# Three graph-attention layers on one core: accumulators kept per head in 28-word rows, heads turned by VectorE, products over padded head rows, index lists loaded early

## What is computed

```python
h = (x @ W).reshape(N, H, C)
alpha_s = einsum('nhc,hc->nh', h, a_src); alpha_d = einsum('nhc,hc->nh', h, a_dst)
e = leaky_relu(alpha_s[src] + alpha_d[dst], 0.2)
m = segment_max(e, dst);  ex = exp(e - m[dst]);  den = segment_sum(ex, dst)
out = segment_sum(h[src] * (ex / (den[dst] + 1e-16))[:, :, None], dst) + b
x = relu(out)                                   # three times
x = layernorm(x + ...)                          # once, after the third
```

## Time and profile before

| | us |
|---|---|
| median of 3 runs (8591.4 to 8609.83) | 8601.86 |
| the profiled execution's own time | 8603.82 |
| its span, first to last instruction | 8601.9 |
| POOL busy | 6236.4 |
| PE busy | 5700.5 |
| DVE busy | 4467.6 |
| ACT busy | 3999.8 |

### The profile page before, as it was taken

The page is one execution under the profiler, slowest core; times in us unless marked ns, Lnnn a source line. Parts: engine busy times, 40 slices in busy tenths (PEclk is TensorE's granted clock), DMA queues, the critical chain, the costliest instruction groups (busy, mean ns, idle before and its releaser), DMA issues. The chain is left out here.

```text
span 8601.9 us, 131191 instructions
## 1 busy us (share of the span) xinstructions
PE 5700.5 (66%) x27740; PEld 5045.6 (59%) x27740; DVE 4467.6 (52%) x11640; ACT 3999.8 (46%) x8993; POOL 6236.4 (72%) x6545
## 2 busy tenths in 40 slices
PE   6999997777566666666656666666665666666663
PEld 2488886666555555555545555555554555555553
DVE  8977765555544444444444444444454444444446
ACT  5755554444344444444434444444443444444443
POOL 3677777777577777777667777777757777777775
PEclk7555555555566666666666666666666666666666
DMA  5222222222122222222222222222222222222221
GB/s 161 65 49 49 49 48 46 47 46 46 36 42 42 42 42 42 42 42 42 37 44 42 42 42 42 42 42 42 42 38 42 42 42 42 42 42 42 42 42 32
DMA packets 290250, 394.16 MB, mean 46 GB/s; under 512 B 176392, under 2 KB 183960, under 8 KB 287984
## 3 DMA queue, kind: packets, MB, share of 16 engines
q0 software_dynamic: 206976, 330.75, 20.1%
q1 hardware_dynamic: 61176, 46.25, 2.2%
q10 hardware_dynamic: 22024, 16.47, 0.8%
HBM read 367.38 MB, written 25.63 MB: 46 GB/s over the span
## 5 line engine op out<-in xcount | busy, mean ns | idle before, releaser
L637 POOL DMA_INDIRECT store<-table_a,idx x4851 | 4615.1, 951 | 1556.5 <-issue 1463.3
L1286 PE MATMUL ps<-store,work 128*128 x9744 | 1769.7, 352 | 945.1 <-ACT work L1218 942.5
L1286 PEld LDWEIGHTS ps<-store,work 128*128 128x128 f32 x9744 | 1646.2, 262 | 1132.3 <-issue 1128.1
L1269 PE MATMUL ps<-ident,work 128*128 128x128 f32 x4872 | 1148.9, 409 | 1371.7 <-ACT work L1225 1371.1
L779 POOL DMA_INDIRECT store<-table_m,idx x1617 | 1532.8, 948 | 615.1 <-issue 478.8
L1225 ACT ACTIVATE work<-work,small 128x896 f32<-128x896 f32 x696 | 725.1, 1042 | 2415.4 <-DVE store L1143 2379.3
L1269 PEld LDWEIGHTS ps<-ident,work 128*128 128x128 f32 x4872 | 920.4, 215 | 1453.8 <-issue 1359.3
L1151 DVE CUSTOM_DVE_ANT_0 work<-work,ps 128x896 f32<-128x896 f32 x696 | 756.6, 1087 | 1231.3 <-issue 937.8
L1162 DVE SCALAR_TENSOR_TENSOR work<-dstf,store,select 128x224 f32 x696 | 314.0, 451 | 1891.4 <-SPq L600 1887.5
L1277 PE MATMUL ps<-ident,work 128*128 128x128 f32 x4872 | 1090.3, 395 | 111.8 <-DVE work L1172 111.8
L1277 PEld LDWEIGHTS ps<-ident,work 128*128 128x128 f32 x4872 | 980.6, 217 | 115.4 <-DVE work L1172 115.4
(11 more groups left out here) (251 smaller groups left out, 5029.8 us busy)
## 6 DMA issues: line engine op xcount, KB each, us to landing
store<-table_a,idx POOLq DMA_INDIRECT x4851
store<-table_m,idx POOLq DMA_INDIRECT x1617, 2.5
work<-edge_parts ACTq DMA_DIRECT2D x232, 45.5 KB
edge_parts<-store SPq DMA_DIRECT2D x6, 1617.0 KB, 11.5
work<-edge_parts SPq DMA_DIRECT2D x50, 192.0 KB
table_a<-work SPq DMA_DIRECT2D x12, 606.0 KB, 6.3
work<-table_b ACTq DMA_DIRECT2D x232, 12.0 KB
idx<-in_src_dram SPq DMA_DIRECT2D x116, 28.0 KB, 1.8
```

The source lines that it names most:

```text
L637: pool.indirect_dma_start(rows[:, k % RING, j, 0:width], None, table, bass.IndirectOffsetOnAxis(ap=idx[:, k // CHUNK, at:at + 1], axis=0)) ...
L1269: last = pe.transpose(ps[:, 4 + j // 4, (j % 4) * P:(j % 4 + 1) * P], prob[:, par, j, :], ident[:])
L1286: last = pe.matmul(ps[:, 6 + par, 0:D + 1], probT[:, par, j, :], rows_of(at("slot", 3))[:, j, 0:D + 1], start=(j == 0), stop=(j == TPG - 1))
```

## The change

The accumulator rows shrink to 28 words: the head's 24 channels, the divisor and the three numbers. For that each head has its own divisor column in the gathered row, which grows from 101 to 104 words, and the sums of a step are 100 columns instead of 97. `parts` becomes eight ACTIVATEs on 32 partitions and 25 columns instead of two on 128 and 97; `accumulate` works on 25 columns instead of 97. Between passes `fold`, PE's turn and the bias step are replaced by `normalise`, on DVE in five pieces: divisors, one multiplication into `heads` (32-word rows, 24 used), and a transposition of 32x32 blocks into `XH`, channels of padded heads on partitions. ACT takes the relu in place, and `product` runs over `XH` with weights laid out in the same padded rows. POOL has no part in it. The table is written in nine transfers instead of five. The final stage uses `normalise` in six pieces, ACT's relu, PE's turn back and one addition from PSUM on DVE; POOL's three operations per chunk go. SP loads the first two index lists while the stage ahead of a pass runs (`first_indices`). Ahead of the first pass, POOL clears only the columns that need it instead of all 19800 words, ACT sums a part of the message accumulator, and ACT shares the copies of the first product. In the preparation the weights come as more and smaller transfers.

```diff
-TW = D + 1 + H
+CW = C + 1
+DX = H * CW
+TW = DX + H
 WX = TW + H
 MW = D + 1
-ROW_A = D + 4
+ROW_A = C + 4
+BIG = 19800
+ONE_AT = (H - 1) * WA + C
...
-        store = sb("store", [P, RING * TPG * TW + (NWA + SPARE_A) * ROW_A])
+        store = sb("store", [P, RING * TPG * TW + BIG])
         rows = store[:, 0:RING * TPG * TW].rearrange("p (r j c) -> p r j c", r=RING, j=TPG)
-        XT = sb("XT", [D + 1, NPAD + WA])
+        XH = sb("XH", [P, NPAD + WA])
+        XT = XH[0:D + 1, :]
...
+                    for h in range(H):
+                        load(sp, bias_heads[h * WA:h * WA + C, :], bias[:, h * C:(h + 1) * C].rearrange("l c -> c l"), s_cols)
...
+                    act.wait_ge(s_const, 5)
+                    for l in range(1, LAYERS):
+                        for h in range(H):
+                            load(act, w_heads[h * WA:h * WA + C, l - 1, 0:DX].rearrange("i (g c) -> i g c", c=CW)[:, :, 0:C],
+                                 Wl[l, h * C:(h + 1) * C, :].rearrange("i (g c) -> i g c", c=C), s_heads)
...
+        def first_indices(sp, of):
+            for b in range(2):
+                sp.dma_start(idx[:, b, :], src[:, b * IW:(b + 1) * IW]).then_inc(of[f"idx{b}"], 16)
...
-                    for c in range(2):
-                        load_indices(c, c)
...
-        NEGMAX, BASE, LOGIT = D + 1, D + 2, D + 3
-        acc = big.rearrange("p (w c) -> p w c", c=ROW_A)
+        NEGMAX, BASE, LOGIT = C + 1, C + 2, C + 3
+        acc = big[:, 0:(NWA + SPARE_A) * ROW_A].rearrange("p (w c) -> p w c", c=ROW_A)
+        heads = big[:, BIG - NWA * WA:].rearrange("p (w c) -> p w c", c=WA)
...
-                        a = big[:, bass.ds(at("row", 4) + v * ROW_A, D + 1)]
+                        a = big[:, bass.ds(at("row", 4) + v * ROW_A, CW)]
...
-                        last = nc.scalar.activation(part_sums[:, par, v, :], ps[:, 6 + par, 0:D + 1], ACT.Copy,
-                                                    scale=selects[:, bass.ds(at("table", 3) + WA + v, 1)])
+                        for h in range(H):
+                            of_head = slice(h * WA, (h + 1) * WA)
+                            last = nc.scalar.activation(part_sums[of_head, par, v, :], ps[of_head, 6 + par, h * CW:(h + 1) * CW], ACT.Copy,
+                                                        scale=selects[of_head, bass.ds(at("table", 3) + WA + v, 1)])
...
-                        last = pe.matmul(ps[:, 6 + par, 0:D + 1], probT[:, par, j, :],
-                                         rows_of(at("slot", 3))[:, j, 0:D + 1],
+                        last = pe.matmul(ps[:, 6 + par, 0:DX], probT[:, par, j, :],
+                                         rows_of(at("slot", 3))[:, j, 0:DX],
...
+        def normalise(dve, link, b0, b1):
+
+            w0, w1 = QUARTERS * tiles[b0][0], QUARTERS * (tiles[b1 - 1][-1] + 1)
+            r = rden[:, w0:w1]
+            link(dve.tensor_scalar(r, acc[:, w0:w1, C], 1e-16, None, ALU.add))
+            link(dve.reciprocal(r, r))
+            link(dve.scalar_tensor_tensor(r, acc[:, w0:w1, NEGMAX], FLOOR, r, ALU.is_lt, ALU.mult))
+            link(dve.tensor_tensor(heads[:, w0:w1, 0:C], acc[:, w0:w1, 0:C], r.unsqueeze(2).broadcast_to([P, w1 - w0, C]), ALU.mult))
+            return dve.transpose(XH[:, w0 * WA:w1 * WA], heads[:, w0:w1, :].rearrange("p w c -> p (w c)"))
+
+        PIECES = [(0, 1), (1, 4), (4, 7), (7, 10), (10, NB)]
+        piece_of = {b: p for p, (b0, b1) in enumerate(PIECES) for b in range(b0, b1)}
+        WRITES = [(b, min(b + 2, NB - 1)) for b in range(0, NB - 5, 2)] + [(b, b + 1) for b in range(NB - 5, NB)]
...
+                nc.scalar.activation(other_half, acc_m[0:D, HALF:N], ACT.Copy, accum_out=small[0:D, 41:42]).then_inc(s_half, 1)
+                act.preload_act_table(ACT.Sqrt)
...
-                link(dve.tensor_reduce(total, acc_m[0:D, 0:N], AX.X, ALU.add))
+                link(dve.tensor_reduce(total, acc_m[0:D, 0:HALF], AX.X, ALU.add))
+                dve.wait_ge(s_half, 1)
+                link(dve.tensor_tensor(total, total, small[0:D, 41:42], ALU.add))
...
-                pool.memset(big, 0.0).then_inc(s_zero, 1)
+                pool.memset(acc[:, :, C:], 0.0).then_inc(s_zero, 1)
+                pool.memset(heads[:, :, C:], 0.0)
...
-                    pool.wait_ge(b_sems["s_rden"], 3)
-                    for c in range(NCH):
-                        fold(pool, c, (QUARTERS - 1,)).then_inc(b_sems["s_fold_pool"], 1)
...
-                        act.wait_ge(b_sems["s_turn"], b + 1)
-                        ts = tiles[b]
-                        nc.scalar.activation(XT[0:D, ts[0] * P:(ts[-1] + 1) * P], ps[0:D, b % 4, 0:len(ts) * P], ACT.Relu,
-                                             bias=bias_l[:, 0:1]).then_inc(b_sems["s_x"], 1)
+                        act.wait_ge(b_sems["s_fold"], piece_of[b] + 1)
+                        v = XH[:, tiles[b][0] * P:(tiles[b][-1] + 1) * P]
+                        nc.scalar.activation(v, v, ACT.Relu, bias=bias_l[:, 0:1]).then_inc(b_sems["s_x"], 1)
...
-                    divisors(dve, b_sems["s_rden"])
+                    n = 0
+
+                    def link(ins):
+                        nonlocal n
+                        n += 1
+                        ins.then_inc(b_sems["s_rden"], 1)
+                        dve.wait_ge(b_sems["s_rden"], n)
+
+                    for b0, b1 in PIECES:
+                        normalise(dve, link, b0, b1).then_inc(b_sems["s_fold"], 1)
                     dve.memset(acc[:, :, NEGMAX], FLOOR)
-                    for c in range(NCH):
-                        fold(dve, c, range(QUARTERS - 1)).then_inc(b_sems["s_fold"], 1)
...
-                    def turn(b):
-                        pe.wait_ge(b_sems["s_fold"], b // CHUNKED + 1)
-                        pe.wait_ge(b_sems["s_fold_pool"], b // CHUNKED + 1)
-                        if b >= 4:
-                            pe.wait_ge(b_sems["s_x"], b - 3)
-                        ts = tiles[b]
-                        for t in ts:
-                            last = pe.transpose(ps[0:D, b % 4, (t - ts[0]) * P:(t - ts[0] + 1) * P], folded[:, t, :], ident[:])
-                        last.then_inc(b_sems["s_turn"], 1)
-
                     pe.wait_ge(b_sems["s_weights"], 1)
-                    for b in range(NB + 1):
-                        if b < NB:
-                            turn(b)
-                        if b >= 1:
-                            pe.wait_ge(b_sems["s_x"], b)
-                            if b >= 5:
-                                pe.wait_ge(b_sems["s_stage"], b - 4)
-                            product(pe, b - 1, 4, 4, w_l[:], b_sems["s_product"])
+                    for b in range(NB):
+                        pe.wait_ge(b_sems["s_x"], b + 1)
+                        if b >= 8:
+                            pe.wait_ge(b_sems["s_stage"], b - 7)
+                        product(pe, b, 0, 8, XH, w_l[:], b_sems["s_product"])
...
+                    sp.wait_ge(b_sems["s_cleared"], 1)
+                    first_indices(sp, shared)
+                    for b0, b1 in WRITES:
+                        t0, t1 = tiles[b0][0], tiles[b1 - 1][-1] + 1
+                        sp.wait_ge(b_sems["s_stage"], b1)
                         sp.dma_start(table_rows[:, t0:t1, :], stage[:, t0:t1, 0:TW]).then_inc(b_sems["s_table"], 16)
-                    sp.wait_ge(b_sems["s_table"], 16 * NCH)
+                    sp.wait_ge(b_sems["s_table"], 16 * len(WRITES))
...
+        ENDS = [(0, 1), (1, 4), (4, 7), (7, 10), (10, 12), (12, NB)]
...
-            @block.gpsimd
-            def _(pool):
-                pool.wait_ge(s_row, 2)
-                for c in range(NCH):
-                    t0, t1 = span(c)
-                    v = folded[:, t0:t1, :]
-                    pool.wait_ge(s_last, c + 1)
-                    pool.tensor_tensor(v, v, rowsb[:, 6, :].unsqueeze(1).broadcast_to([P, t1 - t0, D]), ALU.add).then_inc(s_biased, 1)
-                    pool.wait_ge(s_biased, 2 * c + 1)
-                    pool.tensor_scalar(v, v, 0.0, None, ALU.max).then_inc(s_biased, 1)
-                    pool.wait_ge(s_biased, 2 * c + 2)
-                    pool.tensor_tensor(xn[:, t0:t1, :], xn[:, t0:t1, :], v, ALU.add).then_inc(s_res, 1)
+                for b in range(NB):
+                    pe.wait_ge(s_relu, b + 1)
+                    if b >= 8:
+                        pe.wait_ge(s_res, b - 7)
+                    ts = tiles[b]
+                    for t in ts:
+                        last = pe.transpose(ps[:, b % 8, (t - ts[0]) * P:(t - ts[0] + 1) * P], XH[:, t * P:(t + 1) * P], ident[:])
+                    last.then_inc(s_back, 1)
...
+                        a = xn[:, ts[0]:ts[-1] + 1, :].rearrange("p t (h c) -> p (t h) c", c=C)
+                        dve.tensor_tensor(a, a, ps[:, b % 8, 0:len(ts) * P].rearrange("p (k c) -> p k c", c=WA)[:, :, 0:C], ALU.add).then_inc(s_res, 1)
...
-                divisors(dve, s_den)
```

(14 more changed lines are left out.)

183 lines of the change are left out of this document (103 added, 80 removed).

## The result

The changed kernel takes 8716.6 us (median of four runs, 8708.6 to 8732.6), the kernel before 8603.0 beside it: a ratio of 1.0136 (95% interval 1.0118 to 1.0154). It is slower, by 114 us, where 99 us less was predicted. The profiled execution has a span of 8706.7 us, 104.8 more than before.

What follows compares the result with a forecast made beforehand. POOL's issue of gathers was taken to set the three passes (6100 of 8602 us), leaving gains mainly outside. Terms 1.5 + 7 - 13 - 36 - 29 - 30 + 0 = -99.5 against 8601.9, plus 1.9, gave 8504 us; range 8468 to 8570.

Steps and rivals of the forecast that it cites:

- the loop: what is added to ACT: In the passes: eight small `parts` activations take 1.52 us, 1.07 more per step, hidden behind the gathers.
- The cost is 0: In the passes: the longer `parts` on ACT adds 0 us, since the pair's chain stays hidden by 1.9 us.
- The threshold: In the loop: ACT decides only from 0.30 us per activation on, where the pair's chain passes 17.5 us.
- its own chain, 13.6 us a pair: In the loop: ACT and PE's to-and-fro for a pair of steps before the change, 13.6 us against 17.6 of gathers.
- the rival: In the loop: ACT becomes the bound, deciding from 0.30 us per activation; 8719 us, chance 0.11.
- bites earlier: In the loop bound by ACT: POOL's wait for the turned mask comes earlier, as late `copy_probs` delays PE's mask; unpriced.
- First table and preparation: Ahead of the first pass: 13 us gained in the first table, 1.5 lost to more and smaller weight transfers.
- Turns: Between passes: 18 us gained per turn, 36 for two; the drains, counted separately, lose 2.3 us each.
- Final stage with its drain: After the last pass: final stage 54 us instead of 83, 29 gained; its drain loses 2.3.
- Gathers: In the passes: `accumulate` shortens, line 1169 moves, and gathers held under it gain 30 us in all.
- Slow transpositions: In `normalise`: transpositions at twice the rate cost 6.5 us more in three places, 20 together; 8524 us, chance 0.08.
- Loop bound by ACT: In the passes: at 0.33 us per activation a pair is 0.5 us over, costing 185 us; 8719 us, chance 0.11.

Runs made afterwards that it cites:

- e4: Changed kernel with `parts` as eight activations on all 128 partitions and 7 columns, not picking each head's own columns: 8514.6 us, measured once.
- e5: Changed kernel with the two loops of `parts` swapped, so both rows of a head follow each other on the same partitions: 8585.1 us, ratio 0.9997.
- e3: Changed kernel with the scale of `parts` read from a fixed place, filled by one added copy a step, not a run-time address: 8688.6 us, ratio 1.0136.
- e2: Changed kernel with the eight activations of `parts` replaced by two of 128 partitions, not picking each head's own columns: 8481.2 us, ratio 0.9895.
- e6: Changed kernel with `parts` moved to VectorE as four products a step, one per head, output as after: 8489.7 us, ratio 0.9883.
- e9: e6 with VectorE's four products moved from ahead of the wait for landed gathers to behind the mismatch: 9029.7 us, ratio 1.0511.
- e7: Changed kernel with `parts` split: ScalarE copies each head's columns unscaled, VectorE scales both rows in one product: 8634.4 us, ratio 1.0047.

## Why the prediction was wrong

**The step that failed** is "the loop: what is added to ACT", the sentence "Small ones with a run-time address follow each other in 0.19 (4006.48 to 4006.67), so I take 8 x 0.19 = 1.52". The row was read rightly, but it is a pair of instructions that both work on all 128 partitions. The eight of the change go from head to head, so each works on other partitions than the one before, and then the spacing is the whole length of one and a little more: 0.285 for 0.273. That is 2.27 us per step instead of 1.52 (e4 and e5 show the cause; e3 rules the run-time address out). "The cost is 0" became 169 us in the passes.

**The threshold was too high as well.** By its own chain, 13.6 us a pair, even 2.27 would have come to 17.2 and been hidden under 17.5 by a hair; the rival put its deciding point at 0.30 each. The table shows no such point: waits of 1 to 3 us a pass are there at 0.75, and they grow with `parts` without a step. The chain was one pair's, and of an average kind. `weighted_sums` takes 1.80 or 3.31 from one step to the next (at a granted clock of 1.00 and 0.50, TensorE's levels of 2.4 and 1.2 GHz). And the two steps of a pair are not alike: of some 225 waits in the changed kernel 172, with 106 of the 118 us, stand before the first two gathers of one group of the pair, the other 53 before the first gather of the other group. That some pairs lack cover long before the average does fits both, but no run varies it by itself. The prediction said that POOL's wait "bites earlier" and gave it no price.

**What it missed** is the second half of the loss. The forecast knew that a gather begun under VectorE's line 1169 is longer by the overlap less 0.125, and that the change would move that line out of the way. This is right: in e2 and e6 the excess is below the 13 to 14 us of before. In the changed kernel too the price of that line is gone: the gathers that begin under it are 35 us longer than 0.944 in the three passes before, and 1 us after, which is the gain of 30 that was forecast. But the forecast spoke of a hold only for that short operation. The mask sum behind it, 1.09 us long, holds gathers by the same measure; before, its start simply fell behind the gather's. Once POOL waits, the phase between the two changes, and POOL pays for its wait again. The gathers that begin under the mask sum are 1.5 us longer in all before, and 83 after. Less the 34 just named, and with a few us under other operations, these are the 52 of the 169. The Trainium skill (SBUF — State Buffer, "Who interferes with whom") does state that a VectorE instruction with two inputs in SBUF contends with a GpSimd instruction that reads SBUF. The prediction drew only on the sentence about fast modes from that section. The trace agrees with the other if a gather counts as such a read: e9's mask sum has two inputs in SBUF and holds for 0.91 us, and the reduction with one input in PSUM holds nothing. The same section infers that `tensor_tensor` leaves the making of DMA descriptors alone; the gathers held by the mask sum, which is one, decide against that here. Why 0.11 to 0.13 us of an overlap cost nothing no run here shows.

The other terms, against what was measured:

- *First table and preparation*, -11.5: -11.8. The sum takes 3.90 (predicted 3.8), line 1493 takes 0.27, and the MEMSETs are out of the way.
- *Turns*, -36, with drains on the same way: from last gather to first, 79.2 to 64.5 and 77.0 to 61.9, that is -14.7 and -15.2. The first turn alone is 20.3 shorter (predicted 18). The drain ahead of it is 5.7 longer (predicted 2.3): two to three `parts` at 1.8 more each account for it, the same mis-sized number.
- *Final stage with its drain*, -26.7: -22.1. The stage takes 51 where 54 was predicted, but the drain is 10 longer, 38.0 against 28.0. The longer `parts` are one part of that. The other was in no term of the sum: the granted clock is 0.59 in this drain against 0.78 before, and PE is busy 23.3 us in it against 17.8.
- *Gathers*, -30: right for what it described, and hidden in the changed kernel by the new holds. With `parts` off ACT and few holds (e6) the passes are 30 us shorter than before, at a mean of 945 ns; in e2 they are 17 shorter, at 948.
- *Slow transpositions* fell: 1.78 us for 1536 elements is the rate taken.
- *Loop bound by ACT*, worked out at 8719 and given 0.11, is what came: 8716.6. The closeness is partly luck: the price of 185 us came from a spacing of 0.33 and a wait of 0.5 us a pair, while the runs have 0.285 and two effects, 118 and 52 us. The figure of the Trainium skill that stood beside it (ScalarE: Activation LUTs, "Rules for kernel authors": about 0.3 us for an activation and 0.83 ns an element, an estimate of 0.32 for 25) was closer to the 0.285 than the row that I preferred; for 128x7 at 0.153 it is twice too high.

What stays open: which part of POOL's lateness comes from ACT's chain directly, and which from holds that delay the landing of gathers and so the chain itself, was not separated. Only their sum in the trace is known. TensorE's clock was not separated either: in the first pass the granted clock is 0.67 before and in e2, 0.64 in the changed kernel, and 0.69 in e5. A slower PE lengthens the chain, and waits change when PE works, so it can be cause or consequence. A low clock alone does not make waits: e9 has 0.63 in its first pass and waits of 3 us, though its steps are longer.

## What to carry to other kernels

Before costing small instructions by a row, ask whether that row's neighbours touch the same partitions as yours will. Splitting an instruction over heads that sit in partition ranges cost the full length of each part here, so order the parts so that the range changes seldom, or give the work to an engine that is waiting anyway. And where GpSimd issues gathers back to back, look at what VectorE runs at each gather's start: an operation with two inputs in SBUF has to stand between two starts, and any edit that shifts one against the other, on whatever engine, must be costed by that overlap too.

## What the runs showed of the hardware that was not expected

- Activations overlap only on the same partitions: eight of 128x7 are 0.153 us apart (one lasts 0.282), eight of 32x25 with changing ranges 0.285 (one lasts 0.273), and within a head in e5 0.16 to 0.18 (one lasts 0.264). VectorE's four products of 32x50 in e6, each on another range, do not overlap either: (0.87 - 0.206) / 3 = 0.22 us apart, at 0.206 each. No run has such products on one range, so that the range is the reason there is not shown.
- A per-partition scale makes a short activation longer: 0.179 us without it (e7, 32x25), 0.273 with it (32x25).
- A gather begun under a VectorE operation with two SBUF inputs is longer by the overlap less 0.11 to 0.13 us: 0.38 gives 0.27 (e7), 0.61 gives 0.49 (after), 1.03 gives 0.91 (e9). In all the traces together 2037 gathers begin under a mask sum with over 0.15 us of it left. Of the 1875 that begin some 0.044 us or more behind its start, all but one are held by that measure. The 162 that begin closer to its start are not, and that mask sum lasts 1.15 us in place of 1.09. Moving 0.87 us of VectorE work by a few places cost 540 us.
